# Attention of a decoder layer: probabilities transposed by VectorE in blocks and by transfers inside SBUF, instead of by TensorE

## The reference

```python
xn = layer_norm(x, ln_g, ln_b)                       # x: 32 x 112 x 256
cn = layer_norm(context, cln_g, cln_b)               # context: 32 x 375 x 256
q = (xn @ Wq).reshape(b, n, HEADS, DIM_HEAD).transpose(0, 2, 1, 3) * scale   # 16 heads of 64
k, v = jnp.split(cn @ Wkv, 2, axis=-1)               # one k and one v for all heads
sim = jnp.einsum('bhid,bjd->bhij', q, k) + mask[:, None, :, :]
attn = jax.nn.softmax(sim, axis=-1)
out = jnp.einsum('bhij,bjd->bhid', attn, v)
out = out.transpose(0, 2, 1, 3).reshape(b, n, INNER) @ Wout
val, gate = jnp.split(xn @ W1, 2, axis=-1)
out = out + jax.nn.silu(gate) * val @ W2
```

## Time and profile before

| | us |
|---|---|
| median of 3 runs | 1850.46 (1850.06 to 1851.78) |
| profiled execution, span | 1848.1 |
| group 0 starts | 623.3 |
| groups 1, 2, ... 7 start | 747.8, 897.6, 1047.4, 1197.0, 1346.7, 1496.5, 1646.3 |
| last `highest` | 1798.3 |

### The profile page before, as it was taken

One profiled execution on the slowest core, in us unless ns is written; L12 is line 12 of the kernel. 1 busy time (PEld: TensorE's weight loads), 2 busy tenths in 40 slices (PEclk: granted clock), 3 DMA queues, 4 the chain that ended last, 5 costly groups with the idle time before them and its releaser, 6 DMA issues.

```text
span 1848.1 us, 27947 instructions
## 1 busy us (share of the span) xinstructions
PE 1761.8 (95%) x9224; PEld 1020.1 (55%) x9224; DVE 1310.7 (71%) x3971; ACT 918.7 (50%) x2262; POOL 420.3 (23%) x569
## 2 busy tenths in 40 slices
PE   4579999999999998999999999999999999999997
PEld 2356676766767544455545554544555554555466
DVE  6878988988976588476667648747747666765744
ACT  3444553553541465456545545645645654654542
POOL 4868677777872001000000000000000000000000
PEclk8689999999999999999999999999999999999999
DMA  4000000000013343232222222323223322232200
GB/s 132 11 11 11 21 21 11 31 21 27 6 39 111 95 138 103 55 79 73 73 67 72 76 71 65 81 57 80 66 64 79 75 70 68 72 82 58 54 19 21
DMA packets 102318, 109.22 MB, mean 59 GB/s; under 512 B 38592, under 2 KB 95872, under 8 KB 101280
## 3 DMA queue, kind: packets, MB, share of 16 engines
q1 hardware_dynamic: 101712, 106.99, 21.7%
q10 hardware_dynamic: 464, 0.46, 0.1%
HBM read 96.92 MB, written 7.42 MB: 56 GB/s over the span
## 4 chain that ended last, share of the span: by engine, by line
PE 86%; DVE 8%; ACT 2%; DMA 2%; issue 1%; POOL 1%; DVEq 0%; POOLq 0%; ACTq 0%
PE ps L1530 20%; PE ps L1485 9%; PE ps L1492 9%; PE ps L1523 9%; PE ps L1508 8%; PE ps L314 5%; PE ps L440 4%; PE ps L387 4%; PE ps L427 4%; PE ps L405 3%; PE ps L1590 2%; DVE m_u L727 2%; PE ps L373 2%; PE ps L1584 1%; PE ps L1628 1%
## 5 line engine op out<-in xcount | busy, mean ns | idle before, releaser
L1867 DVE CUSTOM_DVE_ANT_0 x_pr<-ps,x_mk 128x375 f32<-128x375 f32 x448 | 227.6, 545 | 306.1 <-issue 238.9
L1739 ACT ACTIVATE x_pT<-ps 125x384 f32<-125x384 f32 x448 | 195.5, 489 | 269.8 <-PE ps L1492 269.2
L1745 ACT ACTIVATE x_pr<-x_pr,x_mx 128x375 f32<-128x375 f32 x448 | 268.2, 608 | 30.4 <-DVE x_mx L1867 30.4
L1492 PEld LDWEIGHTS ps<-ident,x_pr 128*125 128x125 f32 x1344 | 164.5, 187 | 130.9 <-issue 95.7
L1492 PE MATMUL ps<-ident,x_pr 128*125 128x128 f32 x1344 | 205.7, 289 | 2.5 <-DVE x_pr L1876 2.5
L1530 PE MATMUL ps<-x_xn,x_w 128*128 128x448 f32 x512 | 205.7, 543 | 2.1 <-DVE x_ff L1927 2.1
L1485 PE MATMUL ps<-x_kT,x_qT 64*128 64x375 f32 x896 | 202.6, 529 | 4.1 <-DVE x_mx L1867 4.1
L1876 DVE TENSOR_SCALAR x_pr<-x_pr,x_rc 128x375 f32<-128x375 f32 x448 | 170.9, 424 | 8.0
L1508 PE MATMUL ps<-x_pT,x_va 125*64 125x512 f32 (+1 forms) x768 | 158.4, 548 | 0.6 <-ACT x_pT L1739 0.6
L314 PE MATMUL ps<-m_xa,w_in 128*128 128x448 f32 x352 | 148.2, 568 | 6.2 <-ACT m_xa L532 6.2
L1485 PEld LDWEIGHTS ps<-x_kT,x_qT 64*128 64x128 f32 x896 | 67.7, 185 | 126.3 <-issue 114.4
(11 more groups left out here) (195 smaller groups left out, 2867.3 us busy)
## 6 DMA issues: line engine op xcount, KB each, us to landing
x_mk<-in_mask SPq DMA_DIRECT2D x224, 187.5 KB, 2.4
x_cx<-in_context SPq DMA_DIRECT2D x32, 375.0 KB
x_cT<-in_context_turned SPq DMA_DIRECT2D x32, 375.0 KB, 3.3
x_rb<-context_roots SPq DMA_DIRECT2D x32, 187.5 KB, 4.9
m_Rd<-bc_roots SPq DMA_DIRECT2D x8, 448.0 KB, 3.6
x_mixed<-m_x SPq DMA_DIRECT2D x8, 448.0 KB, 4.0
X<-x_mixed SPq DMA_DIRECT2D x8, 448.0 KB, 4.9
m_X<-in_x SPq DMA_DIRECT2D x7, 448.0 KB, 4.0
```

Source lines behind the costliest of these rows:

```text
L1492: last = pe.transpose(bank(2 + e)[0:JP, t * ROWS:(t + 1) * ROWS], pr[:, 2 * (p % SLOT) + e, t * JP:(t + 1) * JP], ident[:, :])
L1739: act.activation(pT[:, 2 * NV * (batch(p) % 2) + 2 * (p % NP % NV) + e, :, :].rearrange("p t s -> p (t s)"), bank(2 + e)[0:JP, 0:JT * ROWS ...
L1745: act.activation(pr[:, k, :], pr[:, k, :], ACT.Exp, scale=-1.0, bias=mx[:, k:k + 1], accum_out=sums[:, k:k + 1]).then_inc(h_e.sem, 1)
L1867: dve.tensor_tensor_reduce(pr[:, k + e, :], bank(e)[:, 0:J], mk[:, p % SLOT, :], -1.0, 3.0e38, ALU.add, ALU.min, mx[:, k + e:k + e + 1]).t ...
```

## The change

Nothing before the attention is touched. In the attention:

- `turn` leaves PE. DVE transposes `x_pr` in blocks of 32 x 32 (`dve.transpose`, 128 x 384 for each head, two steps behind) into `blocks`, one buffer for the first 4 steps of a sequence and one for the last 3. When such a batch is complete, SP moves its 16 quarter-by-quarter pieces from SBUF to SBUF into `x_pT` (`turned_across`, three steps behind): 16 transfers of 32 partitions by 768 or 576 numbers.
- `copies` goes from ACT, and the product by the reciprocal moves from DVE to ACT (`scaled`, one step behind). DVE keeps the reciprocal.
- `scores` makes the four products of two steps in a row into banks 0 to 3, at even steps. Before them PE waits for both steps' queries and for the last `highest` of the pair before.
- `times_v` comes five steps behind instead of three and waits for the 16 transfers. It reads 128-row pieces whose columns lie in runs of 32. The context is cut in 3 pieces of 128, of which 9 rows are zeros at the end.
- The table of places is another one, with the stages of the norms moved too; `x2` and `fs` are gone, and `so` and `xs` are worked in place.
- In the end part the first half's `end_turn`, `end_up` and `end_down` stand before the last `times_v`.

```diff
-RESULT, TOKENS, TOKENS_FIRST, FINAL = (10, 11, 12), (20, 21, 22), (16, 17, 20), {STEPS - 2: (0,), STEPS - 1: (1, 2)}
+RESULT, TOKENS, TOKENS_FIRST, FINAL = (12, 13, 16), (20, 23, 24), (16, 17, 20), {STEPS - 2: (0,), STEPS - 1: (1, 2)}
+BLK = 32
+RB = ROWS // BLK
+JC = 3
+JW = RB * JC * BLK
+LAG = 5
+PARTS = RB * RB
...
+OUT_AT = (0, 3, 5, 6, 7, 8, 9, 10)
+GATE_AT, VALUE_AT = (9, 11, 13, 14, 15, 16, 17, 20), (10, 12, 13, 14, 16, 17, 19, 21)
+UP_AT = (18, 19, 20, 21, 22, 23, 23, 24)
...
+        def turned_across(i, p):
+
+            if p % NP not in (NV - 1, NP - 1):
+                return
+            n = batch(p)
+            part = JC * BLK * width_of(n)
+            sp.wait_ge(h_t.sem, h_t.value(i, 2 * p + 2))
+            hold(sp, h_o, i, n)
+            for r in range(RB):
+                for q in range(RB):
+                    sp.dma_start(pT[BLK * q:BLK * q + BLK, r * part:(r + 1) * part],
+                                 blocks[n % 2][BLK * r:BLK * r + BLK, q * part:(q + 1) * part]).then_inc(l_pt.sem, 16)
...
+                if p >= 3 or not first:
+                    turned_across(*back(it, p, 3))
...
-            hold(pe, h_m, i, 2 * p)
+            for b in range(GB):
+                if p <= NP * b < p + 2:
+                    emptied(pe, made_in(i, b), ("kv", b))
+            hold(pe, h_m, i, 2 * p)
+            for p in (p, p + 1):
+                two_scores(i, p)
...
-        def turn(i, p):
-            for e in range(2):
-                pe.wait_ge(h_n.sem, h_n.value(i, 2 * p + e + 1))
-                hold(pe, h_c, i, 2 * p + e - 1)
-                for t in range(JT):
-                    last = pe.transpose(bank(2 + e)[0:JP, t * ROWS:(t + 1) * ROWS], pr[:, 2 * (p % SLOT) + e, t * JP:(t + 1) * JP], ident[:, :])
-                last.then_inc(h_t.sem, 1)
...
-            pe.wait_ge(h_c.sem, h_c.value(i, 2 * p + 2))
+            m = batch(p)
+            pe.wait_ge(l_pt.sem, l_pt.value(i, 16 * PARTS * (m + 1)))
...
+            turned = pT[:, 0:JW * width_of(m)].rearrange("p (r t w b) -> p r t w b", r=RB, t=JC, b=BLK)
+            for t in range(JC):
                 for e in range(2):
-                    last = pe.matmul(bank(4)[DH * e:DH * e + DH, 0:n * ROWS], va[:, b % 2, t, :], pT[:, k + e:k + 2 * n:2, t, :],
-                                     start=(t == 0), stop=(t == JT - 1))
+                    last = pe.matmul(bank(4)[DH * e:DH * e + DH, 0:n * ROWS], va[:, b % 2, t, :], turned[:, :, t, e::2, :].rearrange("p r n b -> p n r b"),
+                                     start=(t == 0), stop=(t == JC - 1))
...
-        def copies(i, p):
...
+        def scaled(i, p):
+            k = 2 * (p % SLOT)
+            act.wait_ge(h_r.sem, h_r.value(i, p + 1))
+            for e in range(2):
+                act.activation(pr[:, k + e, 0:J], pr[:, k + e, 0:J], ACT.Copy, scale=rc[:, k + e:k + e + 1]).then_inc(h_n.sem, 1)
...
-            dve.wait_ge(h_r.sem, h_r.value(i, p + 1))
+
+        def turn(i, p):
+
+            n, r = batch(p), p % NP
+            w = width_of(n)
+            if r in (0, NV):
+                hold(dve, l_pt, i, 16 * PARTS * (n - 1))
+            to = blocks[n % 2][:, :].rearrange("p (c w b) -> p c w b", w=w, b=BLK)
             for e in range(2):
-                dve.tensor_scalar(pr[:, k + e, :], pr[:, k + e, :], rc[:, k + e:k + e + 1], None, ALU.mult).then_inc(h_n.sem, 1)
+                dve.wait_ge(h_n.sem, h_n.value(i, 2 * p + e + 1))
+                dve.transpose(to[:, :, 2 * (r % NV) + e, :], pr[:, 2 * (p % SLOT) + e, :].rearrange("p (c b) -> p c b", b=BLK)).then_inc(h_t.sem, 1)
```

188 lines of the change are left out of this document (87 added, 101 removed).

## The result

The changed kernel takes **2072.23 us** (median; 2070.40 to 2076.88), the kernel before beside it on the same chip 1851.12 (1850.06 to 1852.46). The ratio is **1.1195** (95% interval 1.1179 to 1.1211): 12% slower, where 1709 us was forecast, 8% faster. Its profiled execution has a span of 2070.5 us, and a mean granted clock of 0.916.

What follows compares the result with a forecast made beforehand. PE's own work was taken to bound the middle and last groups. Savings of 112.5 us in six middle groups, 20 in the last and 8.5 in the first gave a 1707 span, 1709 us median; range 1665 to 1790.

Steps and rivals of the forecast that it cites:

- What leaves PE: PE per group: transposes 21.3 us and scores in fours 4.2, together 25.5; a middle group's PE work becomes 124.2 us.
- 5 + 1.5: PE stalls on DVE in a middle group: 5 us in steps 12 to 17, 1.5 around steps 23 to 27.
- Rival F: PE: fours of scores share nothing more, or values read slower; 1742 us; chance 0.17 together with another case near 1742.
- What comes to DVE: DVE: two transposes take 1.0 us a step where two products took 0.66; a group gains 9.5 us, reaching about 111.
- What comes to ACT: ACT: two scalings replace two copies a step; at most 7 us a group more, hidden by ACT's idle time.
- The transfers: SP's queue: 0.35 us an issue, 16 take 5.6, about 8.1 with landing; just hidden behind PE's work before `times_v`.
- rival C: SP is late at 0.66 us an issue: three batches cost 11.5 us a group; put at 1785 us, chance 0.18.
- The rule on 32 partitions: SBUF transfers: 32 partitions reach 8 of 16 ports; 16 would take 7.2 us instead of 5.6, giving 1744 in all.
- Rival D: SP's issues exceed 149.75 us a group above 0.88 us each, so slower than before; 1955 at 1.0 us; chance 0.06.
- Where DVE is late: Steps 12 to 17: DVE 31.8 us, including 1.06 tanh waits, against PE's 25.4; with steps 23 to 27, group 131.
- Half clock in the middle groups: TensorE's clock in middle groups: a sign that would upset the whole forecast; a 4.5 us wait costs about 3 more.
- Rival B: PE stays the bound everywhere: 124.2 us a group, 27.5 won in the last, 12 in the first; 1659; chance 0.14.

Runs made afterwards that it cites:

- old kernel with ACT's part: Kernel before, PE's transposes and ACT's copies left out, division moved from DVE to ACT between exponentials and the rest of a step: 1800.44 us, ratio 0.9727.
- one-transfer kernel: Changed kernel with each batch moved by one 128-partition transfer instead of sixteen of 32, quarters not exchanged: 1893.07 us, ratio 1.0232.

## Why the prediction was wrong, point by point

**What leaves PE: right for the scores, some 3 us too much for the transposes.** Eight score records take 1.46 us, as the step said. Without the transposes PE's busy time falls by 18.2 us a group and not 21.3. The group becomes 14.6 us shorter, and 21.3 less the forecast's "5 + 1.5" of stall would be 14.8, but that agreement is luck: those stalls were to come from a load on DVE that this run doesn't have. Rival F is out, and so are its values: twelve records take 2.09 and 2.73 us.

**What comes to DVE: right in size.** A transpose of 128 x 384 is 547 ns, two 0.94 us from start to start (1.0 taken). In a middle group the products were 20.7 us of busy time and the transposes are 28.5: 7.8 more, where 9.5 was summed. DVE is busy 103 us a group, under the 111 that were counted with its small gaps.

**What comes to ACT: the size right, the conclusion wrong.** 592 ns for a scaling, 87 us busy of 154. "Hidden, as long as ACT has 40 us of idle time" is the second step that failed: the idle time lay ahead of the exponentials, where ACT waits for DVE, and the scalings stand behind them, between `highest` and tanh. "I keep 1.06" for the gate's wait became 2.23 in the step shown of the old kernel with ACT's part. With the old table this costs 7.4 us a group, though DVE is relieved; in the one-transfer kernel, with DVE's transposes in place, ACT's scalings are worth 2.8.

**The transfers: the step that failed most.** I had the right row (0.625 us for a transfer from SBUF to SBUF) and chose the other (0.35, a mask from DRAM) because of its two dimensions. The measured issue is 0.63. But the larger fault was the form of the sum: at 0.66 my rival C charged 11.5 us a group for batches that come late for `times_v`. With one transfer 21.3 us a group went, and the larger wait had been for another thing: DVE stood 167 us in the span for `x_rb`, PE 62 for the turned probabilities. "The roots now stand behind 16 transfers, `x_rb` comes about 5 us later, hidden in DVE's stalls": DVE stood 7.06 us for it in the place shown, 6.7 us each time in the mean of 25. The Trainium skill ("DMA: Bandwidth & Descriptors", section "Issuing engines are not separate DMA queues") calls the time to initiate a transfer usually small relative to the transfer; here one issue took 0.63 us and its landing 2.1, and sixteen in one queue 10.06: the measurement decides. The rule on 32 partitions that the prediction took from the Trainium skill ("SBUF — State Buffer", section "Door 1: The DMA port swizzle") changed nothing that is seen, since an eighth of the bytes gave the same 10.06 us, a landing of 1.8 and not 2.1, and no faster kernel.

**Rival D was the right side for the wrong reason.** It decided above 0.88 us an issue, where SP's issue times alone fill a group. With 0.63 they fill some 122 us (128 x 0.63, the values' 25, and 16 for the rest by rival C's sum), and the kernel was slower all the same, since SP also stands, and each stand delays all behind it. Its longest in the attention, over the span (the masks for the highest scores, the roots for their landing, the next tokens for the result):

```profile
SPq L1383 <- DVE x_mx L1882: 206.5, 68, 12.4
...
SPq L1418 <- DMA context_roots<-x_st: 85.1, 31, 6.7
SPq L1421 <- DVEq L1971: 66.4, 6, 11.6
```

In the six middle groups SP stands 50 us a group in all, which with the 122 fills 172 of 174.8. A queue that waits for what it feeds is full long before its busy time is.

**Where DVE is late: the sum was of loads, the truth was of order.** I took 6.5 us of stall a group. Without most of SP's part there are 29 (153.5 against 124.2): in the group read 19.5 of idle time on PE, and 9.8 of busy time over the 124.2, at a clock of 0.97. What is shown: about 8 go with the new work of ACT and DVE together, and a group with neither is still 145.7. The table of places is worth about 11 us in the kernel before without transposes, and what was put back of it 3.3 beside the new load. I had summed six steps' work on each engine and compared; the table had been taken as neutral without a look at which pieces it brings side by side. The parts don't add, and how the last 20 us split between table, ACT, DVE, the scores in fours (not tried alone) and the transfer's landing stays open.

**The clock.** "Half clock in the middle groups" stood among what would upset the whole, and came in part: a mean of 0.93 in the middle group shown where SP is waited for, 0.97 with one transfer. PE's busy time in them is 140.1 and 134.0 us for the same records, so of the 20.7 us between these two groups 6.1 are slower products and the rest is idle time. The low stretches stand behind PE's waits. In the kernel before without transposes, where none is over 0.9 us in the middle groups, the group read has 1.00.

**The first group and the end.** I took 116 us for the first group and 50 for the end part. They measured 166 and 65, and with one transfer a batch 129.1 and 58.9. What holds these last two above the forecast was not looked into.

**Slips in the sums.** Rival B wins 25.5 us in the last group (152 - 126.5); the prediction says 27.5 and adds 26. At 0.66 us an issue the sixteen and the landing take 13.0 us and not 12.6. And the cover of the transfers was counted from the transposes alone, while `turned_across` also holds for PE's last read of the one `x_pT`. None of them changes the verdict.

## What to carry to other kernels

Price a DMA by what its queue needs to issue it, taken from the row of the same kind of transfer (here SBUF to SBUF), times the count, and then read off what stands behind it in that queue and who waits for that: the victim here was a small transfer that had nothing to do with the change. When the bounding engine is relieved by 15%, its waits are set by the order in which the others serve it and not by their busy shares: a moved operation is free only if the idle time lies at the place where it is put. And where a change brings a new table of places with it, test the table by itself first: in the kernel before without its transposes, with the same instructions, it cost about 11 us a group, while the new work of two engines was worth 7.8 in the one-transfer kernel.

## What the runs showed of the hardware

- SP takes 0.63 us to issue a transfer of 32 partitions from SBUF to SBUF, 96 KB or 12 KB alike (sixteen in 10.06 us both times), and GpSimd 0.50 for 96 or 72 KB. One of 128 partitions is issued in 0.52 us and lands, with 1536 KB, in 7.2.
- With eight issued by SP and eight by GpSimd at once, SP needs 0.71 us each and not 0.63, and GpSimd 0.49 as alone. The median landing of 96 KB is 4.0 and 3.7 us, where it was 2.1 with SP alone and 2.9 with GpSimd alone.
- The same data to DRAM: 5.7 us to landing for 384 KB, four at a time, and 6.6 for 1536 KB back.
- After 4 us with 0.24 us of products TensorE's granted clock was 0.60 and 0.55 in the next two stretches of 4 us. A shorter wait was followed by a low stretch too: in the one-transfer kernel PE stood 2.13 us before a gate at 1145.70 and was busy 1.87 of the 4 us up to 1146, and the 4 us from there have 0.64. In the kernel before without its transposes, whose waits are at most 0.9 us in the middle groups, the group read has 1.00.
